# Eight batches through four layers on one core: new orders on four engines, and two more bias banks written by ScalarE

## The reference

```python
x = x + _L0_cond_ref(x, zX, zY, zR, 1, 1)      # zX*lap_x + zY*lap_y + zR*y*(1-y), edges reflected
x = x + _L1_cond_ref(x, W1, b1, v, token)      # scores = tanh(x W1 + b1) v; masked softmax pooling over rows
x = x + _L2_cond_ref(x, subject, weight, bias) # y = x W[subject]^T + b[subject], 512 -> 512
x = x + _L3_cond_ref(x, profile, ...)          # z = relu(x Wd + bd); y = x + z Wu + bu; layernorm(y)*g + b
```

## Time and profile before

| | us |
|---|---|
| median of 3 runs | 611.89 (611.86, 611.89, 618.77) |
| profiled execution, its own time | 620.66 |
| its span | 618.9 |

### The profile page before, as it was taken

The page is one execution under the profiler, slowest core; times in us unless marked ns, Lnnn a source line. Parts: engine busy times, 40 slices in busy tenths (PEclk is TensorE's granted clock), DMA queues, the critical chain, the costliest instruction groups (busy, mean ns, idle before and its releaser), DMA issues.

```text
span 618.9 us, 9325 instructions
## 1 busy us (share of the span) xinstructions
PE 574.5 (93%) x2934; PEld 441.4 (71%) x2934; DVE 478.4 (77%) x1168; ACT 335.5 (54%) x587; POOL 323.7 (52%) x279
## 2 busy tenths in 40 slices
PE   8995869999899998999899998999899998999996
PEld 2344756788659875788659885788658886688784
DVE  7536697679966998679956999679977899667456
ACT  4233457455746577465564657456664657445431
POOL 6543291368507673368516684187625684017421
PEclk8589879999999999999899999999999999999999
DMA  5576007693597457793596557892697656122362
GB/s 170 156 247 112 2 18 228 211 191 91 128 333 158 109 104 226 252 204 81 132 316 147 126 119 178 283 199 53 172 263 193 144 119 162 27 68 69 61 127 85
DMA packets 60000, 93.84 MB, mean 152 GB/s; under 512 B 10999, under 2 KB 15607, under 8 KB 59952
## 3 DMA queue, kind: packets, MB, share of 16 engines
q0 software_dynamic: 16544, 29.90, 29.6%
q1 hardware_dynamic: 34192, 46.58, 22.6%
q10 hardware_dynamic: 9216, 16.78, 7.4%
HBM read 61.26 MB, written 31.98 MB: 151 GB/s over the span
## 4 chain that ended last, share of the span: by engine, by line
PE 50%; DVE 37%; issue 7%; ACT 5%; POOL 1%; DMA 1%; SPq 0%; DVEq 0%; ACTq 0%; POOLq 0%
PE y L636 16%; DVE x2f L1451 9%; DVE xd L1316 6%; PE front_ps L672 6%; DVE xu L1284 6%; PE front_ps L695 5%; DVE x L1323 4%; DVE o_sb L1483 4%; PE front_ps L750 3%; PE front_ps L648 3%; DVE wtl L1418 2%; PE front_ps L680 2%; PE front_ps L686 2%; DVE stats L1467 2%; PE front_ps L636 2%
## 5 line engine op out<-in xcount | busy, mean ns | idle before, releaser
L533 POOL TENSOR_TENSOR norm<-norm 128x1 f32<-128x1 f32 x64 | 37.8, 591 | 187.2 <-DVE norm L1478 187.2
L636 PE MATMUL y<-wth,x2h 128*128 128x512 f32 x256 | 103.7, 405 | 10.6 <-DVE wtl L1418 10.6
L551 POOL TENSOR_TENSOR x2l<-x2f,x2h 128x1024 fp32r<-128x1024 f32 x32 | 81.9, 2561 | 45.6 <-ACT x2h L923 31.4
L636 PE MATMUL y<-wth,x2l 128*128 128x512 f32 x256 | 101.0, 395 | 0.0
L636 PE MATMUL y<-wtl,x2h 128*128 128x512 f32 x256 | 100.4, 392 | 0.0
L540 POOL DMA_DIRECT2D out<-o_sb x58 | 68.4, 1214 | 13.8 <-ACT o_sb L1054 10.5
L1467 DVE BATCH_NORM_STATS2 stats<-y 128x6 f32<-128x512 f32 x64 | 44.3, 692 | 39.3 <-PE y L636 39.3
L509 POOL TENSOR_TENSOR xd<-xn 128x1024 f32<-128x1024 f32 x28 | 61.7, 2206 | 24.7 <-DVE x L1323 16.6
L1451 DVE SCALAR_TENSOR_TENSOR x2f<-alb,small,front_ps 128x128 f32<-128x128 f32 x256 | 70.2, 337 | 2.2 <-POOL x2l L551 0.4
L750 PE MATMUL front_ps<-th_pt,x 128*128 128x129 f32 x512 | 68.2, 281 | 2.8 <-DVE x2f L1451 1.8
L750 PEld LDWEIGHTS front_ps<-th_pt,x 128*128 128x128 f32 x512 | 63.7, 191 | 9.3 <-DVE x2f L1451 6.2
(11 more groups left out here) (148 smaller groups left out, 1184.9 us busy)
## 6 DMA issues: line engine op xcount, KB each, us to landing
xn<-in_x SPq DMA_DIRECT2D x32, 512.0 KB, 11.3
out<-x ACTq DMA_DIRECT2D x58, 256.0 KB, 4.4
out<-o_sb POOLq DMA_DIRECT2D x58, 256.0 KB, 5.5
xu<-in_x SPq DMA_DIRECT2D x21, 512.0 KB, 11.0
xu<-in_x POOLq DMA_DIRECT2D x21, 512.0 KB, 7.6
wn<-in_L_cond_weight SPq DMA_DIRECT2D x8, 1024.0 KB, 5.4
wd<-in_L_cond_down_w SPq DMA_DIRECT2D x8, 256.0 KB, 5.3
wu<-in_L_cond_up_w SPq DMA_DIRECT2D x8, 256.0 KB, 4.1
```

Source lines behind the costliest of these rows:

```text
L551: pool.tensor_tensor(x2l[q][:, k, :], x2f[:, k % 2, :], x2h[q][:, k, :].bitcast(F32), ALU.subtract).then_inc(x2l_ready, 1)
L636: ins = mm(dst, lhs, rhs, start=first and q == 0, stop=last and q == len(parts) - 1, skip_group_check=True)
```

## The change

Five things, all in the written orders. POOL's `rest_up` and `bias_rest` for a batch move from between `rest_x2` 1 and 2 to the end of the step before (they are called with `m`). POOL's `left_and_right` of quarter 1 gets a wait for `add_around` of quarter 0. VectorE's layer-0 calls and `rest_w` are put in another order. ScalarE does `centre` 0 and others at other places, and `seed` serves tiles 1 and 7 too, so `linear` makes a bias matmul for tile 0 alone. TensorE's `score_hidden` 0 goes in front of `transpose_x1` 2, and `adapter_up` 1 in front of `score_hidden` 1.

```diff
-        SEEDED = (3, 4, 5, 6)
+        SEEDED = (1, 3, 4, 5, 6, 7)
...
+            def left_and_right_behind(m, c):
+
+                pool.wait_ge(around, NC * (m - 1) + c)
+                left_and_right(m, c)
+
...  (pool, opening)
                     open_slots()
+                    rest_up(m, 1 - q)
+                    bias_rest(m, 1 - q)
...
                 if m is not None:
-                    left_and_right(m, 1)
+                    left_and_right_behind(m, 1)
...
                     rest_x2(n, q, 1)
-                    rest_up(n, q)
-                    bias_rest(n, q)
...
                 if n is not None:
                     root(n, 0)
+                if m is not None:
+                    rest_up(m, 1 - q)
+                    bias_rest(m, 1 - q)
...  (tensor)
-                if t < 2 or t == 7:
+                if t == 0:
                     pe.wait_ge(y_free, NJ * b + before(t, YB) + 1 + CREDIT)
                     mm(y[:, :], rows_on[:, 0, :], bias[:, q, :], start=True, stop=False, skip_group_check=True)
...
                 if m is not None:
+                    score_hidden(m, 1 - q, 0)
                     transpose_x1(m, 1 - q, 2)
-                    score_hidden(m, 1 - q, 0)
                     transpose_x1(m, 1 - q, 3)
                 if n is not None:
                     adapter_up(n, q, 0)
+                    adapter_up(n, q, 1)
                 if m is not None:
                     score_hidden(m, 1 - q, 1)
-                if n is not None:
-                    adapter_up(n, q, 1)
...  (scalar)
             def seed(b, t):
 
+                act.wait_ge(bias_kept, b + 1)
                 act.wait_ge(y_free, NJ * b + before(t, YB) + 1 + CREDIT)
...
                 if m is not None:
                     scale_rows(m, 0)
+                    centre(m, 0)
                 if b is not None:
                     keep_x3(b, 4)
                     store_base(b, 4)
                     seed(b, 5)
-                if m is not None:
-                    centre(m, 0)
...
                     round_x2(n, q, 2)
                 if b is not None:
+                    seed(b, 7)
                     scale(b, 4)
...
                 if m is not None:
+                    scale_rows(m, 2)
                     centre(m, 1)
-                    scale_rows(m, 2)
...
                     round_w(n, 2)
-                if b is not None:
-                    scale(b, 5)
+                    keep_bias(n)
                 if m is not None:
                     scale_rows(m, 3)
+                if n is not None:
+                    seed(n, 1)
+                if m is not None:
                     centre(m, 2)
                     keep_x1t(m, 1 - q, 1)
+                    centre(m, 3)
```

More of the change, by code:

```diff
@@ L1083, in program @@
                     store_last(2)
-                    for t in range(5, NJ):
+                    keep_last_x3(5)
+                    seed(b, 7)
+                    store_last(3)
+                    for t in range(6, NJ):
                         keep_last_x3(t)
@@ L1176, in program @@
                     round_w(n, 2)
+                    keep_bias(n)
+                if m is not None:
+                    scale_rows(m, 3)
+                if n is not None:
+                    seed(n, 1)
+                if m is not None:
+                    centre(m, 2)
+                    keep_x1t(m, 1 - q, 1)
+                    centre(m, 3)
                 if b is not None:
                     scale(b, 5)
-                if m is not None:
-                    scale_rows(m, 3)
-                    centre(m, 2)
-                    keep_x1t(m, 1 - q, 1)
-                if b is not None:
                     scale(b, 6)
-                    scale(b, 7)
                 if n is not None:
-                    keep_bias(n)
                     keep_x3(n, 0)
                     store_base(n, 0)
-                if m is not None:
-                    centre(m, 3)
+                if b is not None:
+                    scale(b, 7)
                 if n is not None:
@@ L1195, in program @@
                 if m is not None:
+                    hidden(m, 0)
                     keep_x1t(m, 1 - q, 2)
-                    hidden(m, 0)
                     keep_x1t(m, 1 - q, 3)
@@ L1547, in program @@
                     add_carry(n, 0, 1)
+                if m is not None:
+                    times_x(m, 0)
+                if n is not None:
                     carry_products(n, 1)
@@ L1563, in program @@
                     subtract_mean(b, 1 - q, 4)
-                if m is not None:
-                    times_x(m, 0)
                 if n is not None:
@@ L1573, in program @@
                     add_carry(n, 3, 1)
-                if m is not None:
-                    diffuse(m, 1 - q, 0)
-                    add_around(m, 1)
                 if b is not None:
@@ L1579, in program @@
                     subtract_mean(b, 1 - q, 5)
+                if m is not None:
+                    diffuse(m, 1 - q, 0)
                 if n is not None:
                     rest_w(n, 0)
+                if m is not None:
+                    add_around(m, 1)
+                if n is not None:
+                    rest_w(n, 1)
                 if b is not None:
@@ L1587, in program @@
                     diffuse(m, 1 - q, 1)
-                    add_around(m, 2)
-                if n is not None:
-                    rest_w(n, 1)
-                    rest_w(n, 2)
                 if b is not None:
@@ L1594, in program @@
                     subtract_mean(b, 1 - q, 7)
+                if n is not None:
+                    rest_w(n, 2)
                 if m is not None:
-                    times_x(m, 2)
-                    diffuse(m, 1 - q, 2)
+                    add_around(m, 2)
                 if n is not None:
@@ L1601, in program @@
                     add_around(m, 3)
+                    times_x(m, 2)
+                    diffuse(m, 1 - q, 2)
+                    times_x(m, 3)
+                    diffuse(m, 1 - q, 3)
                 if n is not None:
@@ L1604, in program @@
                 if m is not None:
-                    times_x(m, 3)
-                    diffuse(m, 1 - q, 3)
                     take_mask(m)
```

## The result

| | before | after |
|---|---|---|
| median of 4 runs, us | 615.33 | 589.69 |
| all runs, us | 611.86, 611.89, 618.77, 620.47 | 585.77, 589.66, 589.73, 596.30 |
| profiled execution, us (span) | 620.66 (618.9) | 585.77 (584.0) |
| VectorE busy, us | 478.4 | 448.2 |
| TensorE busy, us | 574.5 | 555.3 |

The time of after over that of before is 0.9556, 95% interval 0.944 to 0.9672: faster. Against 611.89, the median that the prediction started from, it is 22.2 us. (Runs whose clock was disturbed are left out of the ratio.)

What follows compares the result with a forecast made beforehand. Bound: TensorE, waiting for wtl because VectorE's SBUF operations and POOL's exclude each other. Six steps of 2.5 us (15.0), first step 2.3, last stages 0.8: 18.1 off 611.89 gives 594 us; range 585 to 604.

Steps and rivals of the forecast that it cites:

- (a): POOL's left_and_right 1 waits for add_around 0, which ends 1.2 us sooner; carries of block 1 stay near 418.3; cost nothing.
- (b): POOL's rest_up and bias_rest leave the queue between x2l 1 and 2 for behind tile 0's root; cost nothing.
- (d): VectorE, last carries to add_around 1: one collision left, add_around 1 with POOL's left_and_right 2, ending at 438.7.
- (c): VectorE's last block of carries, with times_x 0 gone from before it, starts at 425.3, over 1.9 us sooner.
- further long forms on VectorE: Sign against the forecast: long VectorE operations other than the one expected long add_around, that of quarter 1.
- (e): TensorE's linear 0: last wtl at 445.7, done at 446.5 instead of 448.1, 1.6 us a step; bounds 0 and 2.9.
- (f): Tile 1's bias matmul leaves TensorE for a hidden ScalarE bank write: 0.23 us a step; tile 7 counted 0.
- (g): TensorE after tile 1: score_hidden 0 fills the time before transpose_x1 2 and 3; waits go, 0.7 us a step (0 to 0.9).
- (h): First step: row weights meet one POOL left_and_right instead of two, 1.6 us; with bias and short waits 2.3 (1.0 to 3.0).
- (i): Last two stages, bound by TensorE: three bias matmuls, 0.7 us, and little else; 0.8 us.
- The clock: Half-clock stretches: a fallen step cost 1.4 us more; the recorded 3.4 us would be priced 1.7; not counted.
- The first rival: No collision at add_around 1, no TensorE wait in linear: 3.8 us a step, 25.9 in all, 586 us; chance 0.20.

Runs made afterwards that it cites:

- third profile of before: The kernel before, unchanged, profiled once more: 607.88 us; opening 35.83, first step 61.48, full steps of 70.12 to 71.49 us.
- the fourth experiment: The changed kernel with POOL's left_and_right 2 also waiting for add_around 1: median 580.88 us, 0.9533 of before, steps of 66.07 to 66.12 us.

## Why the prediction was right, step by step

Forecast were 15.0 + 2.3 + 0.8 = 18.1 us. Measured, against the third profile of before, were 18.2 for the steps, 0.4 for the first step and 0.6 for the tail, 19.2 us; the rest of the 22.1 is 2.7 us of clock and 0.2 of opening. That the sum came this close is in part luck, for its terms missed both ways.

- **What bounds it** was right: blocked operations on the way to `wtl`, one 1.76 us wait of TensorE for it.
- **(a)** right: `add_around` 0 takes 1.28 and the carries of block 1 stand where they stood. Undone, the step is 1.2 us longer. What it does not say is that this rests on ScalarE's `centre` 0 being early; without it 1.3 us a step are lost.
- **(b)**, "Cost nothing", **was wrong**: the move of the rests costs 1.0 us a step. The cover in their new place is not what it was taken for: `rest_up` at 429.84 (458.1 in the old frame) meets VectorE's `wn<-wn,ident`. That is free, because VectorE waits behind it. What costs is that what they leave behind is an earlier `left_and_right` 2, the partner of the collision in (d). I forecast the collision and didn't see that it was (b) that made it.
- **(c)** right: the last carries begin at 396.90, in the old frame 425.1; forecast 425.3.
- **(d)** right: one long form on the way to `wtl`, `add_around` 1, 2.79 us. The sign "further long forms on VectorE" that I named against me did come, in `wn<-wn,ident`, off that way.
- **(e)** right: the last `wtl` block starts at 416.66 and ends at 417.3, in the old frame 445.6 (forecast 445.7); `linear` 0 is over at 446.43 (446.5), for 448.09: 1.66 us, forecast 1.6. The wait for `zh` grew to 0.69 us, above the 0.5 that I named as a sign against me, yet inside the sum.
- **(f)** right: 0.24 us for 0.23.
- **(g)** the mechanism is right, the size too small: 1.11 us for 0.7. From `linear` 1's end to `spread_scores` it took 11.57 us before (451.94 to 463.51) and takes 10.46 now (421.81 to 432.27), with the same work inside. I had added up the idle column, 0.44 + 0.18. TensorE's timeline before shows what that misses:

```profile
452.81 3.60 PE L672 MATMUL front_ps<-x1t,w 128*128 128x512 f32 x8
456.85 1.09 PE L648 MATMUL front_ps<-ident,x 128*128 128x128 f32 x8 [0.44 <-DVE x L1323]
...
459.05 3.70 PE L672 MATMUL front_ps<-x1t,w 128*128 128x512 f32 x8 [0.18 <-ACT x1t L923]
```

  From start to start the first `score_hidden` takes 4.04 us, against 3.43 undisturbed (421.81 to 425.24): 0.61 for a wait of 0.44. The wait of 0.18 stands for 0.34 (0.57 us from the last matmul before it, at 458.48, for 0.23), and that of 1.76 for 1.92. The two waits make 0.95 of the 1.11 us; the other 0.16 isn't assigned. The idle column counts from the end of the last matmul, 0.39 us after its start, while in an undisturbed row the next one starts after 0.23.
- The step: 1.66 + 0.24 + 1.11 = 3.01 us, the difference of these two steps (70.11 and 67.10); over all steps 3.03. Forecast 2.5. Six of them are 18.2 us and not 15.0, and 2.5 of the 3.2 missing are (g).
- **(h)** 2.3 us forecast; 3.5 against the profile that I read, but only 0.4 against the third profile of before. In that one VectorE reached the row weights before POOL began its sums:

```profile
45.73 0.17 DVE L1400 TENSOR_TENSOR small<-small 128x8 f32<-128x8 f32 x1
```

```profile
49.93 5.05 POOL L509 TENSOR_TENSOR xd<-xn 128x1024 f32<-128x1024 f32 x2
```

  0.17 us where the earlier trace rows has 1.87, and TensorE's wait behind it is 3.49, not 6.90; after has 3.49 too. Over all fourteen profiles this wait takes three sizes: 3.5 to 3.6 us where nothing meets; 5.2 to 5.3 in three kernels with POOL's new wait, where one sum stands there; and 6.8 to 6.9 in two of before and in the changed kernel without that wait, where both do. So the 1.6 us of (h) are there when the two engines meet, 6.9 less 5.2, and nothing when they don't, and whether they meet differs between executions of one kernel. The 0.4 us is no clean figure either: the first step of the third profile has 10.2 us at half clock in it, that of after 13.7.
- **(i)** 0.6 for 0.8.
- **The clock** I left out of the sum. Where before falls, after doesn't, and that is worth 1.3 to 1.4 us a time, none to 2.7 us a run. The steps of this kernel show 1.34 us for 3.4 us at half clock (71.49 against 70.15). The Trainium skill, TensorE: Matmul & The Clock Gate, section Terms, puts the loss at about half of the throttled time, which would be 1.7 us (an estimate by that page); the measured 1.34 decides.
- **The first rival** (no collision at (d), 3.8 us a step) is what the fourth experiment made true: 4.0 a step.

**What the sum over the engines shows.** Undone in the changed kernel, VectorE's order is worth 4.3 us a step, TensorE's 1.95, `centre` 0 1.3, POOL's wait 1.2, the seeds 0.24, and the rests' move -1.0: far more in all than 3.03. Added alone to the kernel before, VectorE's order gives 1.9 and POOL's edits 1.7. The parts are interlocked, and the value of one depends on which of the others stand. But for (b), my parts (a) to (g) were right as a walk through one timeline, not as prices of the edits.

**The opening** follows its half-clock time: 35.7 us with none in it, 40.5 with 10.2 (two of the changed kernels), 45.4 with 20.5 and 47.0 with 23.9, that is 0.47 us for each us at 1.2 GHz, in kernels of before and changed ones alike.

**Open:** why the clock stays at half so long in some openings; what sets the length of the first step beyond the meeting of (h) (with a wait of 3.5 us there it is still 61.1 to 63.4 us long); what ScalarE's other moves do, of which only `centre` 0 and the two seeds were undone; and whether the fourth edit together with the third (rests back and the second wait) gives more, which wasn't tried. In the fourth experiment's step TensorE stands idle for 0.39 us.

## What to carry to other kernels

When two engines exclude each other, give the queue of the less pressed one an explicit wait behind the operation of the other that is on the critical path, and let the long form fall where its engine waits next anyway: in the changed kernel the two placements were worth 1.2 and 1.0 us a step, and no work changed. Where another engine was late behind it, in the kernel before with VectorE's order, the same wait was worth nothing. An operation taken out of a queue is also a delay taken out: ask what now starts sooner behind it, and whom it meets. And count a wait from start to start, take what stands in an opening from more than one execution, and don't price interlocked edits one by one.

## What was not expected of the hardware

- A wait of TensorE costs more than its idle column: 0.44 was 0.61, 0.18 was 0.34 and 1.76 was 1.92 us.
- The block between VectorE and POOL does not depend on the size of VectorE's operation: one of 128x8 takes 0.17 or 1.87 us, one of 128x128 0.28 or 1.35.
- After one wait of 1.76 us in an otherwise full stream the clock sometimes falls to half for 3.4 us, in three of 18 full steps, which costs 1.3 to 1.4 us; in 60 full steps whose waits were 1.41 us at most it never did. In a kernel with another wait further on, such a fall cost 0.4 us.
